# One more of nine value taps goes from VectorE to ScalarE and GpSimd, and the taps, products and normalisations of a slab get new places among the twenty jobs

## What is computed

```python
x = x + _L0_conv_ref(_gn(x), ...)   # wavelet-query attention over channels
x = x + _L1_conv_ref(_gn(x), ...)   # two binarised 3x3 convolutions with batch norm
```

```python
kv = jnp.einsum('oc,bchw->bohw', qkv_w, x)
kv = _dw3x3(kv, qkv_conv_w)                 # depthwise 3x3: nine taps
k, v = jnp.split(kv, 2, axis=1)
q = _ssl(x, conv5_w, conv7_w, conv9_w)      # wavelet, depthwise 3x3, inverse wavelet
attn = softmax(normalise(q) @ normalise(k).T * temperature)
out = attn @ v
```

## The kernel before

| row | jobs |
|---|---|
| 0 | 0 u (channel 3 of the body before), 1 kg0, 2 mq0, 3 s1_0, 4 tk0 |
| 1 | 5 kg1, 6 s1_1, 7 mq1, 8 u0, 9 tk1 |
| 2 | 10 kg2, 11 s1_2, 12 mq2, 13 u1, 14 tk2 |
| 3 | 15 kg3, 16 s1_3, 17 mq3, 18 u2, 19 mq4 |

## Time and profile before

### The profile page before, as it was taken

The page is one execution under the profiler, slowest core; times in us unless marked ns, Lnnn a source line. Parts: engine busy times, 40 slices in busy tenths (PEclk is TensorE's granted clock), DMA queues, the critical chain, the costliest instruction groups (busy, mean ns, idle before and its releaser), DMA issues. The chain is left out here.

```text
span 1428.7 us, 36822 instructions
## 1 busy us (share of the span) xinstructions
PE 1182.4 (83%) x12756; PEld 935.9 (66%) x12756; DVE 1011.0 (71%) x1771; ACT 881.4 (62%) x1574; POOL 423.8 (30%) x473
## 2 busy tenths in 40 slices
PE   0999918999999899998999999635999997999900
PEld 0555508999899898998989899512555554555500
DVE  6677407999999798998999988346767654063394
ACT  0677826788887687886888777110442453766383
POOL 6100023445554555545546545102000010000000
PEclk9999959999999899999999999858999999999955
DMA  9976782345444345344445442068777330000079
GB/s 331 417 306 268 301 165 72 95 125 136 111 123 125 95 125 144 90 130 118 109 133 133 97 128 71 26 233 286 275 261 256 101 131 1 0 1 0 0 275 402
DMA packets 148705, 221.26 MB, mean 155 GB/s; under 512 B 115625, under 2 KB 116789, under 8 KB 144193
## 3 DMA queue, kind: packets, MB, share of 16 engines
q1 hardware_dynamic: 137456, 152.26, 35.0%
q0 software_dynamic: 6480, 47.19, 8.7%
q10 hardware_dynamic: 4608, 19.67, 4.0%
HBM read 131.84 MB, written 87.20 MB: 153 GB/s over the span
## 5 line engine op out<-in xcount | busy, mean ns | idle before, releaser
L1674 PE MATMUL b_conv_bank<-b_sign,wsign 128*128 (+1 forms) x1728 | 296.4, 329 | 10.4 <-ACT b_sign L1454 7.9
L757 POOL TENSOR_TENSOR b_vacc<-b_vacc 128x576 f32<-128x576 f32 x128 | 180.2, 1408 | 331.0 <-ACT b_vacc L850 330.2
L1674 PEld LDWEIGHTS b_conv_bank<-b_sign,wsign 128*128 128x128 bf16 x1728 | 168.6, 98 | 141.3 <-issue 29.1
L989 PE MATMUL b_bank<-b_tkh,b_kt 96*96 96x100 f16 x1536 | 225.2, 212 | 2.3 <-DVE b_tml L970 2.3
L991 PE MATMUL b_bank<-b_tkh,b_kt 96*96 96x100 f16 x1536 | 224.7, 212 | 0.0
L990 PE MATMUL b_bank<-b_tkl,b_kt 96*96 96x100 f16 x1536 | 224.6, 212 | 0.0
L989 PE MATMUL b_bank<-b_yh,b_tmh 96*96 96x200 f16 x768 | 197.2, 257 | 32.0 <-DVE b_feat L954 16.7
L947 DVE SCALAR_TENSOR_TENSOR b_value_sum<-b_vin,b_vtaps,b_value_sum 128x576 f32<-128x576 f32 x256 | 206.8, 808 | 0.0
L989 PEld LDWEIGHTS b_bank<-b_tkh,b_kt 96*96 96x96 f16 x1536 | 196.3, 128 | 3.9 <-DVE b_tml L970 2.5
L1473 ACT CAST b_y<-b_conv_bank 128x384 f32 (+1 forms) x192 | 91.2, 477 | 173.5 <-PE b_conv_bank L1674 171.5
L991 PEld LDWEIGHTS b_bank<-b_tkh,b_kt 96*96 96x96 f16 x1536 | 196.5, 128 | 0.0
(11 more groups left out here) (214 smaller groups left out, 2538.7 us busy)
## 6 DMA issues: line engine op xcount, KB each, us to landing
b_vin<-value_projection_scratch SPq DMA_DIRECT2D x32, 686.0 KB, 6.1
value_projection_scratch<-b_vout ACTq DMA_DIRECT2D x24, 784.0 KB, 4.6
keys_scratch<-b_khl SPq DMA_DIRECT2D x24, 784.0 KB, 3.6
b_kt<-keys_scratch SPq DMA_DIRECT2D x128, 147.0 KB, 2.9
b_xraw<-in_x SPq DMA_DIRECT2D x128, 144.0 KB, 4.9
values_scratch<-b_vacc SPq DMA_DIRECT2D x32, 576.0 KB, 3.2
b_values<-values_scratch SPq DMA_DIRECT2D x48, 384.0 KB, 3.9
out<-xs SPq DMA_DIRECT2D x25, 576.0 KB, 6.9
```

The costliest lines, as they stand in the source:

```text
L757: nc.gpsimd.tensor_tensor(whole, whole, room, ALU.add).then_inc(s_padd, 1)
L989: nc.tensor.matmul(out, w_hi, m_hi, start=first, stop=False)
L1674: ins = nc.tensor.matmul(cbank[k % NBK][:, 0:CH].rearrange("p (r c) -> p r c", c=W), p["wsign"][nth // NIMG][:, t * C:(t + 1) * C], padded ...
```

## The change

Tap 3 also becomes a product of ScalarE, in a third turn through the same room, with a third add of GpSimd. VectorE adds five taps of a half (t = 4 to 8), ten for a body. The product's source now takes a row offset as well, since tap 3 is in the second row of the 3 x 3. All semaphore counts follow. The tables get new places: VectorE taps after jobs 0, 1, 4, 6, 9 and 10, 11, 14, 16, 19; ScalarE's products stand before the copies of jobs 2, 4, 7 and 12, 14, 17, its first taps before 1 and 10, its normalisations before 3, 5, 6, 8, its high_x before 11 and 13. On GpSimd the third add follows the second with its edge step or `low_x` steps; no third group of these comes behind it.

```diff
-        NO_TAP = (2, 4, 6, 8, 12, 14, 16, 18)
-        TAPS = 6
-        NORMALISE, HIGH_X = (4, 6, 7, 8), (13, 14)
-        FIRST_TAP, PRODUCTS = (1, 11), (2, 5, 12, 15)
+        NO_TAP = (2, 3, 5, 7, 8, 12, 13, 15, 17, 18)
+        TAPS, MOVED = 5, 3
+        NORMALISE, HIGH_X = (3, 5, 6, 8), (11, 13)
+        FIRST_TAP, PRODUCTS = (1, 10), (2, 4, 7, 12, 14, 17)
@@ add_product (GpSimd)
-                pool.wait_ge(s_prod, i * 4 + (2 * half + n + 1))
+                pool.wait_ge(s_prod, i * (2 * MOVED) + (MOVED * half + n + 1))
@@ body (GpSimd)
-                for n in range(2):
+                for n in range(MOVED):
                     add_product(i, k % 2, 1, n)
-                    if head is not None:
+                    if head is not None and n < 2:
                         edges(head, (k // GPH - 1) % 2, i, k % GPH, n)
                 if how != LAST:
-                    for n in range(2):
+                    for n in range(MOVED):
                         add_product(i + 1, (k + 1) % 2, 0, n)
-                        low_x(i + 1, (k + 1) % 2, n)
+                        if n < 2:
+                            low_x(i + 1, (k + 1) % 2, n)
@@ product (ScalarE)
-                src = vin[:, slot, :].rearrange("p (r c) -> p r c", c=WP)[:, half * HALF:(half + 1) * HALF, t:t + W]
+                src = vin[:, slot, :].rearrange("p (r c) -> p r c", c=WP)[:, half * HALF + t // 3:(half + 1) * HALF + t // 3,
+                                                                          t % 3:t % 3 + W]
@@ tap_product (ScalarE)
-                if t == 2:
-                    act.wait_ge(s_padd, i * 4 + (2 * half + 1))
+                if t > 1:
+                    act.wait_ge(s_padd, i * (2 * MOVED) + (MOVED * half + t - 1))
@@ body (ScalarE)
-                        if n in PRODUCTS[2 - 2 * half:4 - 2 * half]:
-                            tap_product(of, slot, half, 1 + PRODUCTS.index(n) % 2, True)
+                        if n in PRODUCTS[MOVED - MOVED * half:2 * MOVED - MOVED * half]:
+                            tap_product(of, slot, half, 1 + PRODUCTS.index(n) % MOVED, True)
@@ before the first body (ScalarE)
-            for t in (1, 2):
+            for t in range(1, MOVED + 1):
                 tap_product(0, 0, 0, t, False)
@@ tap (VectorE)
-                slot, half, t = k % 2, m // TAPS, m % TAPS + 3
+                slot, half, t = k % 2, m // TAPS, m % TAPS + (MOVED + 1)
-                if t == 3:
-                    dve.wait_ge(s_padd, i * 4 + (2 * half + 2))
+                if t == MOVED + 1:
+                    dve.wait_ge(s_padd, i * (2 * MOVED) + MOVED * (half + 1))
                 if t == 8 and not last:
-                    dve.wait_ge(s_padd, i * 4 + (2 * half + 4))
+                    dve.wait_ge(s_padd, i * (2 * MOVED) + MOVED * (half + 2))
```

More of the change, by code:

```diff
@@ L940, in tap @@
                 part = vsum[:, :, 0:HALF // 2 * W].rearrange("p b (r c) -> p b r c", c=W)
-                if t == 3:
-                    dve.wait_ge(s_padd, i * 4 + (2 * half + 2))
+                if t == MOVED + 1:
+                    dve.wait_ge(s_padd, i * (2 * MOVED) + MOVED * (half + 1))
                 if t == 8 and not last:
-                    dve.wait_ge(s_padd, i * 4 + (2 * half + 4))
+                    dve.wait_ge(s_padd, i * (2 * MOVED) + MOVED * (half + 2))
                 if m or not isinstance(i, int) or i:
                     dve.wait_ge(s_tap, i * (2 * TAPS) + m)
-                nc.vector.scalar_tensor_tensor(whole if t == 8 else part, src, vtaps[:, t:t + 1], whole if t == 3 else part,
+                nc.vector.scalar_tensor_tensor(whole if t == 8 else part, src, vtaps[:, t:t + 1], whole if t == MOVED + 1 else part,
                                                ALU.mult, ALU.add).then_inc(s_tap, 1)
```

## The result

| | before | after |
|---|---|---|
| median, lowest to highest | 1435.38 us, 1433.67 to 1437.09 (4 runs) | 1457.40 us, 1447.04 to 1459.13 (4 runs) |
| profiled execution / its span | 1430.3 / 1428.7 us | 1459.1 / 1457.5 us |
| ratio after : before | | 1.0138, 95% interval 1.0089 to 1.0188 |

The change makes the kernel 1.4% slower, 22.0 us between the medians; the forecast was 1460 in a range of 1440 to 1476. The profiled execution after is the slowest of its four, and one of the four took 1447.04 us; why isn't known.

A forecast was written before the change was run, and what follows sets the result against it. A loop of waits through ScalarE and VectorE was taken to bound the 21 us body. 31 legs of each kind gave 16.7 and 5.6, the start 2.4: 24.7, rounded to 25, on median 1434.8 gives 1460 us, range 1440 to 1476.

The forecast's parts named there:

- Leg F to E: From F, end of VectorE's first tap of a first half, to E, the same of a second half: +0.5 us.
- the idle before job 8: From F to E, VectorE idles some 0.37 us because a normalisation before job 8's copy is no longer covered by a tap.
- The wait of the second product: From F to E, ScalarE's second product, now at job 4, waits 0.2 us for GpSimd's first add.
- VectorE's idle before job 7: From F to E, VectorE's idle before job 7 would be unchanged or larger; it was 0.39 us before.
- Leg E to F: From VectorE's first tap end in a second half to that in the next first half: 10.54 to 10.7, +0.2 us.
- ScalarE's stand at the third product: From E to F, ScalarE's third product waits some 1.4 us for GpSimd's second add, with three copies behind it.
- The start: At the stage's start, the third product waits for the second add, so the lead copies start 2.4 us later.
- The lower bound of 0.3 us a period: Smallest growth of a body, if the second product's wait and the idle before job 8 vanish; +12 us with the start.
- ScalarE's first gram copy of a head: ScalarE's gram copies, in the way of job 11's copy, may add 0.2 us a head; taken as cancelled by the loop's turns.
- TensorE's clock: Rival, chance 0.12: longer bodies idle TensorE more; three to six more clock falls cost 7.5 to 15 us: 1468 to 1475.
- VectorE as the bound: Rival, chance 0.13: two taps leave the loop, -1.46 us a body, other engines' extra work falls into idle time: 1406 us.
- The lock between VectorE and GpSimd: Rival, chance 0.04: GpSimd's spread slips onto VectorE's first tap and they block each other, up to 0.4 us a body: 1472.

The follow-up runs named there:

- the saving alone: The kernel before with VectorE's tap 3 of each half left out and no product in its place: 1408.2 us against 1433.7.
- the run with the adds first: The changed kernel with both low_x pairs one add later in GpSimd's list, from E to F: 1436.4 us (kernel before 1432.4).
- the run with the mended start: The changed kernel with slab 0's third product behind the eight lead copies instead of ahead of them: 1451.9 us (kernel before 1432.4).

## Why the prediction was right

**What bounds the kernel.** Right, and shown: a loop of waits through ScalarE and VectorE, and after the change GpSimd too. Orders that change no engine's work moved the legs by up to 0.9 us and the time by 1.2%, and the body changes by the sum of its legs.

**Leg F to E, forecast +0.5.** Measured +0.52, by the chain forecast. Job 7's copy ends at F + 6.91 instead of F + 6.02, 0.89 later (forecast 0.88), and the idle before job 8, the leg's last, is 0.27 (0.37). The wait of the second product is there, though the profile puts no bracket to it:

```profile
402.07 0.48 ACT L898 CAST b_yh<-b_bank 96x400 f16<-96x400 f32 x1
402.65 0.78 ACT L852 ACTIVATE b_vacc<-b_vin,b_vtaps 128x576 f32<-128x576 f32 x1
```

The product starts 0.58 after such a copy instead of 0.37, and 0.04 after GpSimd's first add ends (401.21 + 1.40): 0.2, as forecast. One sign failed: VectorE's idle before job 7 was to stay or grow. It has gone. VectorE idles 0.78 before job 4 instead (403.94) and comes to job 7's low part (407.14) just as that copy ends (406.44 + 0.68 = 407.12). The sum was right because the two waits are equal there, which I hadn't worked out.

**Leg E to F, forecast +0.2.** Measured +0.25, by the mechanism forecast: second add at E + 4.10 (forecast 4.1), third at E + 7.22 to 8.63 (7.2 to 8.65), VectorE's stand for it 0.26. ScalarE's stand at the third product is 1.14 to 1.24 (some 1.4).

**The start, +2.4.** Measured 2.38.

**The sum.** Two slips of the recorded working don't change its end. The terms of the leg F to E give 0.52, and the sum goes on with 0.54, 0.6 us more in all. The lower bound of 0.3 us a period doesn't follow from its own condition: 0.72 less 0.2 and 0.37 is 0.15, so the bound is +7 us, or 1442, still inside the range.

**What I put at nothing.** 31 bodies of 0.77 give 23.9 us for the stage, and the stage grew by 21.8. What lies between are terms that I put at nothing, or held to cancel, and that they do cancel is luck. ScalarE's first gram copy of a head, ahead of job 11's copy, costs the leg E to F behind it some 0.4 beyond the 0.25 of every leg in the first head and 0 to 0.2 in the later ones, near the 0.2 that I gave it. Two of these seven legs are longer still, 11.46 and 11.43: TensorE's clock fell in them, where the kernel before had none. On the other side the kernel before had two falls that the changed one hasn't: at 560 us and at 820 us. The legs there took 23.55 and 23.60 before and 21.76 and 21.74 after, while other bodies grew by 0.77, so the two are worth 2.6 us each. A row of the kernel before, then one of the changed kernel:

```profile
820.00:825.00 5.00, 5.00 (x50) 5.00 (x49) 3.02 (x6) 1.16 (x2) 0.78 (x2) 0.50 0.47 143
437.00:440.00 3.00, 3.00 (x20) 2.75 (x19) 2.71 (x5) 1.77 (x5) 3.00 (x4) 0.50 0.37 87
```

The first leg E to F took 14.00 instead of 12.49; there the clock fell after a stop of 3.4 us (3.0 us before the change, with no fall):

```profile
242.00:245.00 3.00, 2.78 (x18) 2.81 (x19) 0.81 (x1) 0.00 (x0) 0.93 (x3) 0.57 0.40 155
```

The granted clock is 0.57 in the mean of these 3 us, mostly 1.2 GHz, and job 0's 18 matmuls took 2.8 us, where the 18 of job 18 just ahead of the stop took 1.6 at full clock. In sum: forecast 24.7 for stage and start, measured 24.2. Why the clock falls at some bodies in one kernel and at others in the other stays open.

**The rivals.** VectorE as the bound (0.13) is refuted by the saving alone: even with no product in its place the tap was worth 0.36 of 0.73 in one leg and 0.63 in the other. That kernel took 1408 us in its one execution, so 1406 is near what the change would bring if ScalarE and GpSimd did their part for nothing; they cost more than the taps save. The rival's cap of 21.0 us for a body with all gram parts was wrong, as the row of 20.51 shows. The rule that the forecast took from the Trainium skill, Perfetto Trace Analysis, section Optimizing Scalar/DVE Operations, on moving work from a saturated VectorE, was the one that spoke for 1406. The trace doesn't bear it out here: busy time was no sign of what ended the body. TensorE's clock (0.12) added less than it took away, by the falls above. The lock between VectorE and GpSimd (0.04) didn't act in the changed kernel: its taps F last 0.81, all of them. It acts as soon as the two meet, as the run with the adds first shows, and there the tap's own length grew by 0.22 a body where I had allowed up to 0.4.

## What to carry to other kernels

When in-order engines hand work round in a loop, find the points at which each starts just as the one before ends, and add up the legs between them; an engine busy 92% of the time can still be one that waits. Work moved to a less busy engine costs its full length there if copies that others wait for stand behind it, and a further turn through the same room adds a handshake: here a cost of 1.5 us a body for a saving of 1.0, each measured alone. Before moving work between engines, move it along the list of one: that gave 1.2% here.

## What the runs showed of the hardware

- A VectorE scalar_tensor_tensor with two SBUF inputs and a GpSimd tensor_tensor hold each other up. The tap went from 0.81 to 1.03 us when it began 0.41 us before the end of a low_x, and the spread that came next went from 0.46 to 0.99; moved apart, both were back at 0.81 and 0.47. In the run with the mended start a first tap that began under a spread, the only one, took 1.01. The taps whose second input is b_value_sum, which is in PSUM, overlapped GpSimd's adds and low_x (in the kernel before 383.03 + 0.81 beside 382.41 + 1.79) and kept 0.81. The wait shows in the length of the record and not as a gap before it. The Trainium skill, SBUF — State Buffer, section Terms, describes the shared pair of ports as held for the full instruction, the other engine fully blocked. The trace agrees that the two exclude each other in part; that the tap grew by 0.22 and not by the 0.41 of overlap leaves the full block unshown.
- A row in which TensorE is busy throughout isn't one in which it sets the time: the same body took 21.00 us with 327 matmuls and 20.51 with 324, busy for all of it both times.
- GpSimd starts 0.17 to 0.19 us after the product that releases it ends (389.47 + 0.78, then 390.43), ScalarE 0.02 to 0.05 after its releaser, VectorE 0.02 to 0.04 after ScalarE. VectorE's last tap, which waits for GpSimd's third add, starts 0.11 to 0.13 after it in most bodies (396.65 + 1.41, then 398.19). Each turn product, add, product thus costs some 0.2 us beside its work.
- With the same code behind the stage, that part took 528 to 542 us in fourteen executions. Differences of a few microseconds in single runs are best read in the stage that was changed.
